# Rounded scores for the maxima, the second causal mask on GpSimd, and a new step table with zero products

## What is computed

```python
x = x + conv_attention(group_norm(x))          # layer 0: 4 heads of 32, RMS norm over channels, no mask
t = tokens(x)
t = t + causal_attention(layer_norm(t))        # layer 1: 4 heads of 16, causal mask over 256 tokens
t = t + moe_ffn(layer_norm(t))                 # 8 experts, 64 -> 256 -> 64, exact GELU, top 2 by a softmax gate
```

## Time and profile before

| | |
|---|---|
| runs, median (lowest to highest) | 114.87 us (114.58 to 115.00) |
| the profiled execution | 114.85 us |
| its span, first to last instruction | 112.8 us |
| PE busy | 101.8 us (90%) |
| PE weight loads busy | 52.8 us (47%) |
| DVE busy | 75.4 us (67%) |
| ACT busy | 65.1 us (58%) |
| POOL busy | 15.8 us (14%) |

### The profile page before, as it was taken

One profiled execution on the slowest core, in us unless ns is written; L12 is line 12 of the kernel. 1 busy time (PEld: TensorE's weight loads), 2 busy tenths in 40 slices (PEclk: granted clock), 3 DMA queues, 4 the chain that ended last, 5 costly groups with the idle time before them and its releaser, 6 DMA issues.

```text
span 112.8 us, 2251 instructions
## 1 busy us (share of the span) xinstructions
PE 101.8 (90%) x831; PEld 52.8 (47%) x831; DVE 75.4 (67%) x210; ACT 65.1 (58%) x121; POOL 15.8 (14%) x28
## 2 busy tenths in 40 slices
PE   5989978889899999997899998999999999999920
PEld 2346456655555455566666654675342323232300
DVE  6965899979505469999966688998638453155250
ACT  4039973433888756564329958894937644764400
POOL 7900200000000000000000000000003941343140
PEclk9999999999999999999999999999999999999999
DMA  2940000199700000000000000000000000000003
GB/s 74 246 84 7 2 0 9 31 237 189 118 0 0 0 9 0 0 0 0 6 0 6 0 0 0 0 0 3 0 6 0 0 0 0 0 0 0 0 0 93
DMA packets 6633, 3.16 MB, mean 28 GB/s; under 512 B 4432, under 2 KB 6496, under 8 KB 6624
## 3 DMA queue, kind: packets, MB, share of 16 engines
q1 hardware_dynamic: 5936, 2.38, 11.5%
q10 hardware_dynamic: 688, 0.66, 2.3%
HBM read 2.77 MB, written 0.26 MB: 27 GB/s over the span
## 4 chain that ended last, share of the span: by engine, by line
PE 68%; DVE 16%; ACT 10%; issue 3%; DVEq 0%; ACTq 0%
PE bank L933 13%; PE bank L944 13%; PE bank L874 6%; PE bank L807 6%; PE bank L839 5%; PE bank L888 4%; PE bank L858 4%; PE bank L749 3%; PE bank L758 3%; PE bank L721 2%; DVE mx L590 2%; DVE mx L586 2%; ACT sq L399 2%; PE bank L845 1%; ACT sq L405 1%
## 5 line engine op out<-in xcount | busy, mean ns | idle before, releaser
L481 ACT ACTIVATE hid<-bank,b1c 128x1024 f32<-128x1024 f32 x16 | 16.9, 1112 | 11.8 <-PE bank L933 11.8
L437 ACT ACTIVATE pr<-bank 128x1024 f32<-128x1024 f32 (+1 forms) x16 | 14.0, 914 | 8.5 <-PE bank L845 5.1
L933 PE MATMUL bank<-xn,w_sb 64*128 64x512 f32 x64 | 15.6, 612 | 0.0
L944 PE MATMUL bank<-hid,w_sb 128*64 128x512 f32 x64 | 15.3, 603 | 0.0
L705 DVE SCALAR_TENSOR_TENSOR yw<-bank,b2c,wc 128x512 f32<-128x512 f32 x8 | 6.0, 748 | 12.6 <-PE bank L944 12.6
L721 PE MATMUL bank<-still 128*128 128x512 bf16 (+1 forms) x41 | 11.8, 437 | 1.2 <-DVE still L495 1.2
L359 POOL TENSOR_TENSOR acc<-yw,x 64x512 f32<-64x512 f32 x1 | 1.3, 1269 | 72.1 <-DVE yw L705 72.1
L586 DVE TENSOR_REDUCE mx<-bank 128x4 f32<-128x1024 f32 x8 | 9.3, 1218 | 0.9 <-PE bank L807 0.8
L807 PE MATMUL bank<-k,q 32*128 32x256 f32 (+1 forms) x128 | 8.3, 373 | 1.6 <-ACT q L425 0.6
L933 PEld LDWEIGHTS bank<-xn,w_sb 64*128 64x128 f32 x64 | 5.6, 186 | 8.5 <-ACT hid L481 4.4
L364 POOL TENSOR_TENSOR acc<-acc,yw 128x512 f32<-128x512 f32 x6 | 7.6, 1274 | 11.8 <-DVE yw L705 11.6
(11 more groups left out here) (148 smaller groups left out, 176.4 us busy)
## 6 DMA issues: line engine op xcount, KB each, us to landing
w_sb<-in_L_ffn_W_dram SPq DMA_DIRECT2D x3, 512.0 KB, 7.2
x<-in_x_dram ACTq DMA_DIRECT2D x2, 256.0 KB, 4.8
xg<-in_x_dram SPq DMA_DIRECT2D x1, 256.0 KB, 3.2
wg<-in_L_conv_w_qkv_dram SPq DMA_DIRECT2D x2, 96.0 KB, 4.8
bqkv<-in_L_attn_b_qkv_dram SPq DMA_DIRECT2D x12, 0.1 KB, 1.6
wo1t<-in_L_attn_W_out_dram SPq DMA_DIRECT2D x8, 4.0 KB, 1.8
out_dram<-acc SPq DMA_DIRECT2D x1, 128.0 KB, 2.5
out_dram<-acc ACTq DMA_DIRECT2D x1, 128.0 KB, 2.8
```

Of the source, the lines that this page charges most:

```text
L437: nc.scalar.activation(pr[:, b, 2 * p:2 * p + 2, 0:n], two(key, 0, n), ACT.Exp, scale=SCALE[l]).then_inc(free(key), 1)
L481: nc.scalar.activation(hid[:, k % 4, :, :], two(("h", 0, k)), ACT.Gelu, bias=b1c[:, k:k + 1]).then_inc(free(("h", 0, k)), 1)
L933: i = mm(ps(key, i=s), w1_sb[r, e, P * j:P * j + P], XN[r, 2 * s:2 * s + 2, :].rearrange("p b t -> p (b t)"), start=True, stop=True)
L944: i = mm(ps(key, p0=C * s, p1=C * s + C), w2_sb[:, k, :], hid[:, k % 4, s, :], start=(j == 0), stop=(j == FT - 1))
```

## The change

Scores for the maxima: POOL copies Q and K of each image to float32r tiles (`qr`, `kr`, new steps), and `scores` multiplies these. `mx`, the maxima, are float32r too, and `turn` is a plain product with a float32r identity.

```diff
+            def qr(l, b):
+                emptied(pool, ("yq", l, b))
+                nc.gpsimd.tensor_copy(Qr[:, b, :], Q[:, b, 0:T]).then_inc(S["qr", l], 1)
+
+            def kr(l, b):
+                emptied(pool, ("yk", l, b))
+                nc.gpsimd.tensor_copy(Kr[:, b, :], K[:, b, 0:T]).then_inc(S["kr", l], 1)
...
-                emptied(pe, ("yq", l, b))
-                emptied(pe, ("yk", l, b))
+                idle(("s", l, b, 0), ZEROS["scores", l][b])
+                pe.wait_ge(S["qr", l], b + 1)
+                pe.wait_ge(S["kr", l], b + 1)
...
-                        i = mm(bank_of("s", l, b, h)(c, c + n), Q[rows(h), b, P * q:P * q + P], K[rows(h), b, 0:n],
+                        i = mm(bank_of("s", l, b, h)(c, c + n), Qr[rows(h), b, P * q:P * q + P], Kr[rows(h), b, 0:n],
...
-                    i = nc.tensor.transpose(ps(key, P * q, P * q + P), mx[l][:, b, q, :, :].rearrange("p h c -> p (h c)"), ident[:, :])
+                    i = mm(ps(key, P * q, P * q + P), mx[l][:, b, q, :, :].rearrange("p h c -> p (h c)"), identr[:, :],
+                           start=True, stop=True)
```

```diff
+            def causal(l, b, p):
+
+                emptied(pool, ("t", l, b, p))
+                diag = pr[:, b, 2 * p:2 * p + 2, :].rearrange("p h (n c) -> p h n c", c=P)[:, :, 0:3:2, :]
+                nc.gpsimd.affine_select(out=diag, in_=diag, compare_op=ALU.is_ge, fill=0.0, base=0,
+                                        pattern=[[0, 2], [0, 2], [1, P]], channel_multiplier=-1).then_inc(S["causal", p], 1)
...
-                if l:
-                    for h in range(H):
-                        i = mm(blocks(bank_of("t", l, b, h)(0, L1)), identb[:, :], twice(cmask[:, 1, :]), start=False, stop=True,
...
+                    idle(key, ZEROS["num", l][b])
                     for p in range(2):
-                        emptied(pe, ("t", l, b, p))
+                        pe.wait_ge(S["causal", p], b + 1)
```

```diff
+            pool.wait_ge(stats, 2)
...
+            pool.wait_ge(S["xn", 0], 1)
+            nc.gpsimd.memset(V1[:, :, :, :, :], 1.0).then_inc(padded, 1)
```

The table: every place and bank is new, each line has a fifth entry, the zeros ahead of that step for each image, and there are steps for the weight preparation (`prepa`, `prept`, `prepb`) and for half products of the FFN (`uphalf`). The zeros are placed behind `claim` and ahead of the step's other waits. They come to 64 besides the 13 at the start, where they were 28, 8 of them of half width. Lines of layer 1:

```diff
+    ("scores", 1, (124, 144, 171, 181), ((2, 6), (0, 2), (2, 6), (2, 0)), (0, 0, 1, 5)),
+    ("max0", 1, (130, 152, 176, 186), (), ()),
+    ("max1", 1, (143, 163, 178, 190), (), ()),
+    ("turn", 1, (148, 167, 183, 194), ((6,), (0,), (6,), (0,)), (0, 1, 0, 2)),
+    ("shift", 1, (150, 172, 185, 197), (), ()),
+    ("again", 1, (159, 175, 189, 201), ((0, 6), (0, 4), (4, 2), (2, 0)), (4, 0, 0, 0)),
...
+    ("gate", 2, (240, 251, 262, 263), ((5,), (5,), (5,), (4,)), (0, 0, 0, 1)),
+    ("logits", 2, (244, 261, 264, 265), (), ()),
+    ("uphalf", 2, (253, 256, 260), ((0,), (2,), (6,)), (0, 1, 0)),
```

```diff
+            def up_part(k, n):
...
+                pe.wait_ge(S["xn", 2], 2 * n + 2)
+                e, j = divmod(k, FT)
+                for s in range(2):
+                    r = slice(C * s, C * s + C)
+                    i = mm(ps(key, T * n, T * n + T, i=s), w1_sb[r, e, P * j:P * j + P], XN[r, 2 * n + s, :],
+                           start=(n == 0), stop=True, skip_group_check=True)
...
-            up(0)
-            up(1)
+            for k in range(3):
+                up_part(k, 1)
             pe.wait_ge(ld["w2"], 16)
             for e in range(E):
-                if e + 1 < E:
+                if e == 0:
+                    up(3)
+                elif e + 1 < E:
                     up(FT * e + 2)
                     up(FT * e + 3)
+                if e == E - 1:
+                    last()
+                    break
```

```diff
+            dve.wait_ge(shuffled, E)
+            e = E - 1
+            for n, key in enumerate((("y", 0, e), ("z", 0))):
+                cols = slice(T * n, T * n + T)
+                filled(dve, key)
+                if n == 0:
+                    dve.wait_ge(summed, e)
+                nc.vector.scalar_tensor_tensor(yw[:, e % 2, cols], ps(key, 0, T), b2c[:, e:e + 1], wc[:, e % 2, cols],
+                                               ALU.add, ALU.mult).then_inc(free(key), 1)
+                dve.wait_ge(summed, E)
+                emptied(dve, key)
+                nc.vector.tensor_tensor(acc[:, cols], acc[:, cols], yw[:, e % 2, cols], ALU.add).then_inc(result, 1)
```

More of the change, by code:

```diff
@@ new lines @@
+    ("max0", 0, (30, 38, 67, 73), (), ()),
+    ("max1", 0, (34, 45, 70, 76), (), ()),
+    ("turn", 0, (39, 48, 77, 84), ((6,), (2,), (2,), (0,)), (0, 1, 0, 0)),
+    ("shift", 0, (40, 52, 79, 94), (), ()),
+    ("again", 0, (43, 58, 81, 99), ((6, 4), (0, 4), (6, 2), (2, 6)), (3, 0, 0, 0)),
+    ("exp0", 0, (49, 64, 85, 106), (), ()),
+    ("exp1", 0, (54, 68, 89, 110), (), ()),
+    ("den", 0, (69, 74, 104, 113), ((0,), (1,), (0,), (1,)), (2, 0, 0, 0)),
+    ("num", 0, (72, 78, 109, 118), (), ()),
@@ L102, in hybrid_block @@
     ORDER = [(step, l, b, banks[b] if banks else ()) for _, step, l, b, banks in
-             sorted((place[b], step, l, b, banks) for step, l, place, banks in PLAN for b in range(B))]
+             sorted((at, step, l, b, banks) for step, l, place, banks, _ in PLAN for b, at in enumerate(place))]
+    ZEROS = {(step, l): zeros for step, l, _, _, zeros in PLAN}
     seat, nth, follows = {}, {}, {}
@@ L138, in hybrid_block @@
             take(("logits", l, b), banks[0])
-    for k in range(NK):
-        take(("h", 0, k), 2 * (k % 3), 2)
-    take(("gate_t", 0), 7)
+        elif step == "uphalf":
+            take(("h", 0, b), banks[0], 2)
+    for k in range(3, NK):
+        take(("h", 0, k), seat["h", 0, k % 3], 2)
+    last_pair = 12 - sum(seat["h", 0, k] for k in range(3))
+    take(("gate_t", 0), last_pair + 1)
     for e in range(E):
-        take(("y", 0, e), 6 + e % 2)
+        take(("y", 0, e), last_pair + e % 2)
+    take(("z", 0), seat["h", 0, NK - 3])
     with ExitStack() as ctx:
@@ L190, in hybrid_block @@
         V1 = sb("v1", [P, B, KT, H, 32])
-        mx = [sb(f"mx{l}", [P, B, KT, H, 32]) for l in range(2)]
+        mx = [sb(f"mx{l}", [P, B, KT, H, 32], F32R) for l in range(2)]
+        Qr = sb("qr", [P, B, T], F32R)
+        Kr = sb("kr", [P, B, T], F32R)
+        identr = sb("identr", [P, P], F32R)
         mrow = sb("mrow", [P, B, T], F32R)
@@ L269, in hybrid_block @@
         S = {(n, l): sem(f"{n}{l}") for l in range(3) for n in ("dev", "sq", "lnv", "r0", "rs2", "xr", "t2", "xn")}
-        S |= {(n, l): sem(f"{n}{l}") for l in range(2) for n in ("shifted", "lden", "rden", "dr", "a", "att")}
+        S |= {(n, l): sem(f"{n}{l}") for l in range(2) for n in ("causal", "qr", "kr", "shifted", "lden", "rden", "dr", "a", "att")}
         spread1 = sem("spread1")
@@ L635, in logits @@
                 emptied(dve, key)
-                for t in range(KT * b, KT * b + KT):
+                for t in range(first, first + KT):
                     i = nc.vector.max(m8[:, t, :], lg[:, t, :])
@@ L698, in _ @@
             spread(1)
-            for e in range(E):
+            for e in range(E - 1):
                 key = ("y", 0, e)
@@ L896, in gate, with up @@
                     i = mm(ps(key, E * t, E * t + E), XN[:, b, P * t:P * t + P], wgate[:, :], start=True, stop=True)
+                i.then_inc(full(key), 1)
+            def up_part(k, n):
+                key = ("h", 0, k)
+                if n == 0:
+                    claim(pe, key)
+                    idle(key, ZEROS["uphalf", 2][k])
+                pe.wait_ge(ld["w1"], 32)
+                pe.wait_ge(S["xn", 2], 2 * n + 2)
[4 more added lines that the diff above has]
+                           start=(n == 0), stop=True, skip_group_check=True)
+                if n:
+                    i.then_inc(full(key), 1)
+            def up(k):
+                key = ("h", 0, k)
+                claim(pe, key)
+                e, j = divmod(k, FT)
+                for s in range(2):
+                    r = slice(C * s, C * s + C)
+                    i = mm(ps(key, i=s).rearrange("p (b t) -> p b t", b=2), w1_sb[r, e, P * j:P * j + P], XN[r, s:s + 3:2, :],
+                           start=True, stop=True)
                 i.then_inc(full(key), 1)
```

222 lines of the change are left out of this document (113 added, 109 removed).

## The result

The changed kernel takes 120.33 us (119.83 to 121.19) where the kernel before takes 114.72 us on the same chip: a ratio of 1.0495, 95% interval 1.0463 to 1.0527. The forecast was 111.5 us, with a range of 108.9 to 114.3. The profiled execution took 120.31 us.

A forecast was written before the change was run, and what follows sets the result against it. PE was taken to bound most of the kernel, with DVE's maxima and copies setting the pace in layer 1 from 44.2 to 56.4 us. The sum was 114.85 - 1.0 - 1.1 - 1.05 - 0.2 = 111.5 us, range 108.9 to 114.3.

The forecast's parts named there:

- walk: Layers 0 and 1 stepped through by row durations: layer 1's first scores at 42.2 us, last maximum at 59.6.
- The start: First scores wait for POOL's copies and end at 15.8 us, 0.2 us late in place of 0.6 early.
- Term A: Layers 0 and 1 up to the last weighted sum, ending at 66.2 us where it was 67.17: -1.0 us.
- Term B: From the last weighted sum to the FFN: 8.5 us where it took 9.6, -1.1 us.
- Term C: FFN: first halves of three up-products go into pauses, with 0.46 us of wait for the first GELU: -1.05 us.
- Term D: Tail: last add ends 1.66 us behind PE's end, was 1.57; smaller last stores save 0.3: -0.2 us.
- (a): Rival: PE is the bound throughout, so all saved PE time pays: 108.1 us; chance 0.15.
- (b): Rival: POOL and DVE block each other in layer 1, six waits of 0.45 us, +2.7: 114.2 us; chance 0.13.
- (c): Rival: PE's clock falls where PE waits more, from 44 to 60 us; two falls cost 5.65: 117.1; chance 0.10.
- (d): Rival: the rounded products are no faster, losing 0.5 at the start and about 0.9 in layer 1: 112.9; chance 0.04.

The follow-up runs named there:

- n_fix: Changed kernel with its scores' and second products' zeros moved between bank claims, and weight preparation's read and image 1's logits earlier: 116.66 us, ratio 1.0174.
- b_causal: Kernel before with only the POOL select in place of the four causal mask products: 114.48 us, ratio 0.9979.
- o_newops: All new operations of the changed kernel in the kernel before's step order, with only the old zeros: 113.17 us, ratio 0.987; a fourth execution 120.88.
- best2: Same kernel as `best` with two more zeros between the bank claims of image 1's scores: 112.19 us, ratio 0.9785.
- after: The changed kernel itself, as profiled after the change: 120.33 us, ratio 1.0495 against the kernel before.
- b_round: Kernel before with only the rounded scores (POOL copies, rounded products and turn): 116.57 us, ratio 1.0167.
- n_nozeros: Changed kernel with 50 of its 64 table zeros taken out: 116.52 us, ratio 1.0148.
- o_clock: New operations in the old order plus nine zeros where PE waits in layer 0: 116.26, 116.13, 116.29 and 113.21 us.
- o_fp32: New operations in the old order, but scores in float32 without POOL's copies: 114.29 us, ratio 0.9967.
- best: New operations in the old order, zeros between claims in both layers, one second half before the last gate, both last-expert halves weighed before adding: 112.79 us, ratio 0.9822.
- b_round_z: Kernel before with only the rounded scores, plus 15 zeros between bank claims and at image 2's projection: 113.92 us, ratio 0.9934.
- b_zeros: Kernel before with 50 of the change's zeros put behind the claims of the same steps: 122.46 us, ratio 1.0697.

## Why the prediction was wrong

**Where the zeros stand.** This is the step that failed first. The prediction put the 45 added zeros between 0 and 10.8 us, found 2 us of them in its walk, and took those as part of a gain. The upper end, 10.8 us more, was then in no case: its own range went up to 113.1 by the POOL operations alone, and the one slower case was the clock, where the zeros stood as an argument *against* it. They are placed behind `claim` and ahead of the step's other waits, and the question not asked was which wait of a step is the long one. In `scores` and `again` it is the claim, so they come behind the pause. Measured: 3.6 us by place alone, 7.9 of 10.8 in the old order.

Forecast and measurement are 8.8 us apart. By the medians 3.7 of these are the zeros' place together with the two late readers (`n_fix`), 3.5 are the new order as it then stands against the old one, and 1.7 are what the same operations in the old order miss of 111.5.

**The start.** The copies came at 14.61 to 15.34, where 14.25 to 15.15 was predicted, and 0.40 each, where 0.45 was taken. But the scores started at 17.0 and not at 15.1, because of a bank and not of an operand: ACT's last copy out of it ended at 16.19, and the step's two zeros stood behind. The prediction went through the queues of POOL and SyncE and not through ACT's, where `prepb` is. It is worth 1.6 us at that place and, with the logits, 1.75 in the end. The statistics took 0.69 us, as forecast.

**Layer 0 and 1 by hand.** The walk put layer 1's first scores at 42.2 (measured 47.2; 44.6 with both repairs; 43.3 in the old order) and the last maximum at 59.6 (67.0; 63.2; 58.9). The pause named in the text, image 2's shift behind image 3's scores, is there: 2.50 us of DVE. It was judged to leave the maximum "hardly before now", and the repaired kernel is 3.4 later than before. **Term A** (-1.0) was +7.4: the last maximum ends 7.2 us late, the last exponential starts 6.3 late (71.1 against 64.8), and the last weighted sum ends at 74.5 in place of 67.2. That sum does not wait for a select, as was foretold: the select ends at 72.6, and PE comes to the sum at 73.65 from other products. The old order shows what the operations bring here: its last weighted sum ends at 66.2, as forecast, but the microsecond is won ahead of the last maximum (58.9 against 59.8) and not behind it, where the prediction had PE free sooner. **Term B** (-1.1) was right: from the last weighted sum to the last normalised image the trace has 8.3 us, against 9.6 before and 8.5 in the prediction.

**Term C** (-1.05) was +0.1. PE's wait for the GELU was counted at 0.46 and is 0.44. But the count of what stands ahead of that GELU held one gate, and there are two with a zero (1.19 us), for the bank that late logits hold. Even with one gate the halves win nothing: PE needs 31.2 us from the last normalisation to its end in the old order with halves, as before. The chain there is gate, one half, GELU, and halves pay only when one is issued ahead of the gate.

**Term D** (-0.2) was -0.4. The first add waits for POOL (0.73 us) as said, the last add ends 1.8 behind PE's end where 1.66 was predicted, and the smaller store on ACT's queue takes 2.2 us in place of 2.8, a gain of 0.6 where 0.3 was allowed.

**The rivals.** (a) is refuted: with the order kept and the clock held, the operations bring 1.5 of its 6.75 us. (b) is refuted as the cause of the loss, but its mechanism is real. In the changed kernel DVE paid nothing: its `xn` operations took 0.425 us in the mean and the last operation of `weigh` 0.426, as before. In one place POOL paid:

```profile
67.87 0.43 DVE L660 SCALAR_TENSOR_TENSOR att<-dr,att 128x256 f32<-128x256 f32 x1
...
67.99 0.80 POOL L381 TENSOR_SCALAR_AFFINE_SELECT pr<-pr 128x512 f32<-128x512 f32 x1 [4.80 <-ACT pr L482]
```

The select starts 0.12 us behind DVE's operation and takes 0.80 us, where the others take 0.63 to 0.64. In the old order it is DVE that starts second and pays: 0.78 in place of 0.43 us in `b_causal` (rows above), in `o_newops` and in `best2`, each time once and on the chain. The Trainium skill, "SBUF — State Buffer", Who interferes with whom, has a DVE instruction with two SBUF inputs and a GpSimd one that reads SBUF wait for each other; these rows agree. So does the row that the prediction held against it: the subtraction of 0.32 us overlapped the select by only 0.18 us, and with no select beside it (`after`, 2.60 us) it takes 0.28. What was wrong is the size, six waits of 0.45 on DVE in layer 1: there were none here, and one of 0.35 in the old order.

(c), the clock, was not what made the changed kernel slow (1.00 throughout in the profiled execution): "slower" had 0.11 in the forecast nearly all for this cause, and that it came out slower doesn't bear it out. But the fall is real: it came in most executions of `b_round`, `n_nozeros` and `o_clock` and in some of `o_newops`, `o_fp32` and `best`. A fall of 6.8 us cost 2.1 us (`b_round` against `b_round_z`, the profiled executions) and one of 10.2 cost 3.0 (`o_clock`). At 0.10 it was priced too low for a kernel without the zeros and at the wrong cause for this one. (d) is refuted: an image's scores take 0.43 to 0.49 us in the chain. The select took 0.66 in the mean, below the 0.9 taken.

## What to carry to other kernels

Products of zeros that are to fill a pause must be issued ahead of the wait that makes the pause, into a bank that is free already; behind it they are work on the critical path at nearly full price (7.9 of 10.8 us here). So list, for each step, its waits in order and which of them ends last, before placing anything among them. When a step is moved, look for the reader of the bank that it held (`prepb`, `logits`) as well as for its operands, and when a change halves an engine's work in a thin stretch, look at the granted clock there before counting the gain. And when work moves to POOL, look at which of DVE's operations with two inputs in SBUF it will run beside, and which of the two starts second.

## What the runs showed of the hardware

**The clock.** TensorE's granted clock fell to 0.50 (1.2 GHz) in the middle of kernels in which PE was never idle for long. The traces have the fall at 17.1 us for 6.8 us (`b_round`), at 19.3 for 6.8 (`n_nozeros`), at 53.2 for 10.2 (`o_clock`) and at 20.2 for 3.4 (`best`). PE was busy for 2.35 of 4.00 us ahead of the first and 1.64 of 3.00 ahead of the third. The longest single pause of PE in the 6 us ahead of these falls was 1.15, 1.36, 1.05 and 0.60 us. But the changed kernel has pauses of 1.30 and 1.41 us between 15.3 and 18.9 us and kept 1.00. So the length of one pause doesn't decide it, and what does is not shown. The Trainium skill, "TensorE: Matmul & The Clock Gate", A second HAM failure mode, describes such a fall from idling a little between groups of products; the rows of the four falls agree. With fifteen zeros, 3.2 us of product, mostly in pauses, `b_round_z` had 0.994 or more in all five executions.

The fall isn't the same in each execution: the new operations in the old order had 0.996 or 0.997 three times and 0.913 once, at 7.7 us more.

**DVE and POOL.** Fourteen of the traces (all but those of the kernel before and of `b_zeros`) have DVE operations with two inputs in SBUF beside selects or float32r copies of POOL, 70 pairs in all. In each pair the one that started second took longer by their overlap less 0.14 us (to within 0.03), and the one that started first was not made longer by it; pairs that overlapped by less than that show nothing. Examples are 0.43 us that became 0.78 with 0.51 of overlap (DVE), and 0.64 that became 0.80 with 0.31 of overlap (POOL).

**POOL's durations.** A select over 512 columns takes 0.64 us with nothing beside it, and one over 128 columns 0.29 (`after`; the 0.34 of the earlier trace rows ran beside DVE's operations); a copy of 256 columns to float32r takes 0.40, against 0.29 for a copy of 128. As an estimate from these four, that is a fixed part of some 0.2 us and a bit under 1 ns for each column.
